# A selective scan and a routed expert block on one core: dt's softplus moved out of PSUM, convolution taps on VectorE in three chunks, and a new interleaving of the steps

## What is computed

```python
xz = x @ W_in.T;  xc, z = split(xz)
xconv = xp[:, :-2]*conv_w[:,0] + xp[:, 1:-1]*conv_w[:,1] + xp[:, 2:]*conv_w[:,2]
xs = silu(xconv);  x_dbl = xs @ W_x.T            # dt_param 64, Bp 16, Cp 16
dt = softplus(dt_param @ W_dt.T + b_dt) + 1e-5
s_t = exp(-exp(A_log) * dt) * s_{t-1} + Bp * dt * xs     # 256 channels x 16 states
out = ((Cp @ W_C.T) * s_t.sum(-1) + D_param * xs) @ W_out.T * silu(z)
```

## Time and profile before

| what | value |
|---|---|
| median of 3 runs | 1205.05 us |
| the profiled execution, its own time | 1197.84 us |
| its span, first to last instruction | 1196.0 us |
| mean granted TensorE clock | 0.907 |
| scans of chunk 0 begin, scans of chunk 7 end | 36.1 us, 658.0 us |
| busy: PE, DVE, ACT, POOL | 85%, 56%, 54%, 57% |

### The profile page before, as it was taken

One profiled execution on the slowest core, in us unless ns is written; L12 is line 12 of the kernel. 1 busy time (PEld: TensorE's weight loads), 2 busy tenths in 40 slices (PEclk: granted clock), 3 DMA queues, 4 the chain that ended last, 5 costly groups with the idle time before them and its releaser, 6 DMA issues.

```text
span 1196.0 us, 15402 instructions
## 1 busy us (share of the span) xinstructions
PE 1013.7 (85%) x4654; PEld 821.6 (69%) x4654; DVE 670.1 (56%) x1152; ACT 643.6 (54%) x1238; POOL 685.4 (57%) x666
## 2 busy tenths in 40 slices
PE   5437497878876878977988899999999999999996
PEld 3204265656655656765776678889999999998885
DVE  6999997998998989955995332100110000110332
ACT  4776769777486695667754443233333333333342
POOL 0696958777489897598696447453243333322221
PEclk9667588898787988898998999999999999999998
DMA  9110100202002016121464659598999988863511
GB/s 293 57 36 1 61 11 18 71 12 77 1 18 71 1 45 221 45 75 62 112 195 110 181 139 237 103 295 247 358 358 332 291 278 264 271 181 62 176 62 53
DMA packets 141636, 163.91 MB, mean 137 GB/s; under 512 B 26345, under 2 KB 126977, under 8 KB 141537
## 3 DMA queue, kind: packets, MB, share of 16 engines
q1 hardware_dynamic: 125872, 144.20, 37.2%
q0 software_dynamic: 15680, 18.72, 8.2%
HBM read 136.57 MB, written 26.74 MB: 137 GB/s over the span
## 4 chain that ended last, share of the span: by engine, by line
PE 49%; POOL 13%; DVE 13%; issue 12%; ACT 7%; SPq 2%; DMA 2%; DVEq 0%; POOLq 0%; ACTq 0%
PE psum L1107 21%; PE psum L1074 9%; PE psum L1063 6%; PE psum L1086 6%; POOL Ssum L1700 6%; DVE S L1292 6%; POOL list_d L1719 2%; DVE psum L1267 2%; ACT A L1570 2%; PE psum L948 1%; PE psum L1050 1%; PE psum L1009 1%; DMA bb<-b 1%; PE psum L1029 1%; POOL xs L1675 1%
## 5 line engine op out<-in xcount | busy, mean ns | idle before, releaser
L1700 POOL TENSOR_TENSOR Ssum<-Ssum,S 128x512 f32<-128x512 f32 x240 | 303.6, 1284 | 89.2 <-DVE S L1292 88.3
L1107 PE MATMUL psum<-w,hT 128*128 128x256 f32 x1136 | 257.1, 384 | 11.7 <-issue 9.2
L1107 PEld LDWEIGHTS psum<-w,hT 128*128 128x128 f32 x1136 | 216.5, 193 | 43.0 <-issue 10.6
L1750 POOL DMA_INDIRECT acc_d<-y,ID x71 | 112.5, 1584 | 231.8 <-DMA acc_d<-y,ID 115.1
L1570 ACT ACTIVATE A<-dts,nea 128x512 f32<-128x512 f32 x256 | 175.0, 717 | 73.8 <-DVE S L1292 61.7
L1074 PE MATMUL psum<-XT,w 128*128 128x256 f32 x800 | 186.1, 390 | 12.5 <-issue 6.2
L1267 DVE TENSOR_TENSOR psum<-us,psum 128x512 f32<-128x512 f32 x256 | 163.3, 683 | 52.1 <-PE psum L993 51.6
L1074 PEld LDWEIGHTS psum<-XT,w 128*128 128x128 f32 x800 | 154.9, 195 | 40.7 <-issue 10.7
L1292 DVE TENSOR_TENSOR_SCAN S<-A,carry,psum 128x512 f32<-128x512 f32 x120 | 148.6, 1266 | 0.0
L1063 PE MATMUL psum<-nT,s 128*128 128x256 f32 x512 | 134.7, 421 | 10.8 <-DVE nb L1305 10.3
L1292 DVE TENSOR_TENSOR_SCAN S<-A,psum 128x512 f32<-128x512 f32 x120 | 141.2, 1206 | 2.4 <-POOL Ssum L1700 2.3
(11 more groups left out here) (162 smaller groups left out, 1222.9 us busy)
## 6 DMA issues: line engine op xcount, KB each, us to landing
w<-W SPq DMA_DIRECT2D x92, 1024.0 KB, 7.0
bb<-b SPq DMA_DIRECT2D x46, 128.0 KB, 8.0
xnb<-x SPq DMA_DIRECT2D x16, 256.0 KB, 3.0
Xr<-x SPq DMA_DIRECT2D x16, 256.0 KB, 4.6
x_d<-gb SPq DMA_DIRECT2D x8, 512.0 KB, 2.9
xn_d<-nb SPq DMA_DIRECT2D x8, 512.0 KB, 3.3
X<-x_d SPq DMA_DIRECT2D x16, 256.0 KB, 7.8
ACC<-acc_d SPq DMA_DIRECT2D x16, 256.0 KB, 5.0
```

Source lines behind the costliest of these rows:

```text
L1107: t = eng.matmul(bank(g)[:, 256 * k:256 * k + 256], hT[n % 2][:, f, 128 * k:128 * k + 128], w[:, f, :], start=f == 0, stop=f == 7)
L1700: eng.tensor_tensor(to, to, of, ALU.add).then_inc(nsum, 1)
L1750: eng.indirect_dma_start(acc_d, bass.IndirectOffsetOnAxis(ap=ID[:, col, 1:2].bitcast(u32), axis=0), y[n % NY][:, k, :], None, compute_op=A ...
```

## The change

Seven edits, made together:

1. `prep` begins 3 slots before the end of the chunk before (FIRST_PREP = -3) and has one yield more between `silu` and `dbc`. In chunk 2's list, silu goes from slot 11 to 9 and dbc from 15 to 14; the beside gelu goes from slot 8 to 4.
2. Softplus works in SBUF (tile `us`), so `dt_out` gives the two banks back at slots 19 and 20. ScalarE adds 1e-5 there in an extra Identity per half.
3. `dt_sum` of chunks 1 to 7 goes from VectorE to GpSimd.
4. The taps of chunks 5, 6 and 7 are added by VectorE out of PSUM; ScalarE's two extra copies and GpSimd's two additions per half fall away there.
5. `low_out` and the steps by it are moved: softplus directly behind `low`, `low_out` three slots later, behind `nT_out`.
6. The scratch of `top2`, `weigh` and `place` lies in the PSUM bank that `count` uses, taken from `top2` on; weigh and place have one instruction more each.
7. `room()` lets an `up` through with 3 of 5 banks open; `table` steps take 1.5 slots instead of 2 while the scans run; "beside" gets 58 calls instead of 54.

Where the steps stand then: before, 18 groups have their gelu ahead of `direct()` and the tiles t8 to t12 run in it; now 19, and t9 to t12. Of the `up` and `down` steps, 14 more stand ahead of the last scan, all of them in chunks 5 to 7.

The 24 table steps have two pairs of scatters among them, where they had one pair of gathers and one of scatters. The diff, cut to its core:

```diff
-FIRST_POST, LAST_POST, FIRST_PREP, LAST_PREP = 0, 27, 0, 27
+FIRST_POST, LAST_POST, FIRST_PREP, LAST_PREP = 0, 27, -3, 27
...
     def room():
 
-        while len(open_uses) > room_for[0] - (2 if past[0] else 3):
+        while len(open_uses) > room_for[0] - 2:
             yield
...
             say("xc_out", i, 0, x0)
             yield
             say("z", i, 0, z0)
-            say("conv", i, 0, x0)
+            if not conv_by_dve(i):
+                say("conv", i, 0, x0)
             say("xc_out", i, 1, x1)
             yield
             say("z", i, 1, z1)
-            say("conv", i, 1, x1)
+            say("conv", i, 0 if conv_by_dve(i) else 1, x0 if conv_by_dve(i) else x1)
             say("z_out", i, 0, z0)
             yield
+            if conv_by_dve(i):
+                say("conv", i, 1, x1)
             say("z_out", i, 1, z1)
             yield
             say("silu", i)
+            yield
             yield
             yield
             yield
@@ -185,28 +189,27 @@
         say("dt", i, 1, t1)
         if i:
             say("dt_out", i, 0, t0)
+            yield
+            say("dt_out", i, 1, t1)
             say("mid_out", i)
-            yield
-            say("low", i)
-            say("dt_out", i, 1, t1)
         else:
             say("mid_out", i)
             say("dt_out", i, 0, t0)
             say("dt_out", i, 1, t1)
-            say("low", i)
-        yield
-        say("softplus", i, t0, t1)
+        yield
+        say("low", i)
+        say("softplus", i)
+        yield
+        yield
+        yield
         say("low_out", i)
...
             say("load_x", i + 1)
         if not i:
             say("stats_x", 6)
-        for c, t in enumerate((t0, t1)):
-            say("dt_sum", i, c, t)
+        for c in range(2):
+            say("dt_sum", i, c)
             say("u", i, c)
...
-        say("top2", r)
+        g = next(use)
+        say("top2", r, g)
         yield
         if not past[0]:
         say("soft", r)
-        g = next(use)
         say("count", r, g)
         yield
         yield
-        say("weigh", r)
+        say("weigh", r, g)
         say("place", r, g)
         yield
...
         for n in range(2 * len(ROUND[r])):
...
             if not past[0]:
                 yield
-                yield
-            elif n % 2:
+            if n % 2:
                 yield
...
+    ahead, done_prep = prep(1), 0
+
+    def prepare(k):
+
+        nonlocal done_prep
+        want = min(n_prep, -(-n_prep * (k + 1 - FIRST_PREP) // (LAST_PREP + 1 - FIRST_PREP)))
+        part(ahead, want - done_prep)
+        done_prep = max(want, done_prep)
+
     for i in range(NC):
-        ahead = prep(i + 1) if i + 1 < NC else iter(())
         behind = post(i - 1) if i else iter(())
-        done_post = done_prep = 0
+        done_post = 0
         for k, _ in enumerate(main(i)):
             tick()
             if k >= FIRST_POST:
                 want = min(n_post, -(-n_post * (k + 1 - FIRST_POST) // (LAST_POST + 1 - FIRST_POST)))
                 part(behind, want - done_post)
                 done_post = max(want, done_post)
-            if k >= FIRST_PREP:
-                want = min(n_prep, -(-n_prep * (k + 1 - FIRST_PREP) // (LAST_PREP + 1 - FIRST_PREP)))
-                part(ahead, want - done_prep)
-                done_prep = max(want, done_prep)
+            if k == LAST_PREP + 1:
+                part(ahead, 99)
+                ahead, done_prep = prep(i + 2) if i + 2 < NC else iter(()), 0
+            if k <= LAST_PREP or k >= 32 + FIRST_PREP:
+                prepare(k if k <= LAST_PREP else k - 32)
             part(routing, 1)
             if i:
 
-                calls = 54 if listed[0] else 26
+                calls = 58 if listed[0] else 26
                 part(beside, calls * (k + 1) // 32 - calls * k // 32)
         part(behind, 99)
-        part(ahead, 99)
...
-TAKING = {"xT", "nT", "xc", "z", "dbc", "dt", "cmat", "wout", "logit", "count", "turn", "up", "down"}
-GIVING = {"xT_out", "nT_out", "xc_out", "z_out", "dbc_out", "dt_sum", "yadd", "gated", "lg_out",
+TAKING = {"xT", "nT", "xc", "z", "dbc", "dt", "cmat", "wout", "logit", "top2", "count", "turn", "up", "down"}
+GIVING = {"xT_out", "nT_out", "xc_out", "z_out", "dbc_out", "dt_out", "yadd", "gated", "lg_out",
           "place", "turn_out", "up_out", "down_out", "weighed"}
 
-TOP, WEIGH, PLACE = 14, 3, 7
+BY_DVE = {0, 5, 6, 7}
+
+
+def conv_by_dve(i):
+    return i in BY_DVE
+
+
...
     if step == "dt":
-        return "dt_done", 2 * i + n + 1
+        return "dt_out", 4 * i + 2 * n if i else n + 1
...
+        def scratch(r, g):
+
+
+            w, b = len(ROUND[r]), bank(g)
+            ranks, eq, oh1 = (b[:, 8 * w * n:8 * w * (n + 1)].rearrange("p (j e) -> p j e", e=8) for n in range(3))
+            mx, ix = (b[:, (24 + n) * w:(25 + n) * w] for n in range(2))
+            return w, ranks, eq, oh1, ohs[:, 0:w, :], mx, q2[:, 0:w], ix
 
...
-                        p = xs[0][:, c, :]
-                        eng.wait_ge(xc_out, taps(0, c))
+                    if conv_by_dve(i):
+                        p = xs[i % 2][:, c, :]
+                        eng.wait_ge(xc_out, taps(i, c))
                         eng.scalar_tensor_tensor(p[:, 1:512], bank(g)[:, 0:511], cw[:, c, 0:1], p[:, 1:512],
                                                  ALU.mult, ALU.add).then_inc(conv, 1)
-                        eng.wait_ge(conv, 2 * c + 1)
+                        eng.wait_ge(conv, 4 * i + 2 * c + 1)
                         eng.scalar_tensor_tensor(p[:, 0:511], bank(g)[:, 1:512], cw[:, c, 2:3], p[:, 0:511],
                                                  ALU.mult, ALU.add).then_inc(conv, 1)
                 elif step == "dbc_out":
@@ -1250,10 +1267,11 @@
                     if i == 0:
...
                 elif step == "dt_sum":
-                    i, c, g = a
-                    eng.wait_ge(softp, 4 * i + 3 + c)
-                    eng.scalar_tensor_tensor(dts[i % 2][:, c, :], bank(g), 1e-5, dts[i % 2][:, c, :],
-                                             ALU.add, ALU.add).then_inc(dt_done, 1)
+                    i, c = a
+                    if i == 0:
+                        eng.wait_ge(softp, 3 + c)
+                        eng.scalar_tensor_tensor(dts[0][:, c, :], us[0][:, c, :], 1e-5, dts[0][:, c, :],
+                                                 ALU.add, ALU.add).then_inc(dt_done, 1)
...
+                    r, g = a
+                    w, pr, eq, oh1, oh2, mx, m2, ix = scratch(r, g)
+                    logits = lg[:, ROUND[r].start:ROUND[r].stop, :]
                     eng.wait_ge(lg_out, ROUND_END[r])
                     if r:
                         eng.wait_ge(soft, r)
+                    if BEFORE[g] is not None:
+                        name, value = BEFORE[g]
+                        eng.wait_ge(emptying[name], value)
                     one(top, eng.memset(M[:, w, :], 0.0))
-                    best(logits, mx, oh1[:, 0:w, :], w)
-                    one(top, eng.scalar_tensor_tensor(pr[:, 0:w, :], oh1[:, 0:w, :], -3e38, logits, ALU.mult, ALU.add))
-                    best(pr[:, 0:w, :], m2, oh2[:, 0:w, :], w)
-                    one(top, eng.tensor_tensor(M[:, 0:w, :], oh1[:, 0:w, :], oh2[:, 0:w, :], ALU.add))
-                    one(top, eng.tensor_tensor(dd[:, 0:w], m2[:, 0:w], mx[:, 0:w], ALU.subtract))
+                    for score, m, oh in ((logits, mx, oh1), (pr, m2, oh2)):
+                        if oh is oh2:
+                            one(top, eng.scalar_tensor_tensor(pr, oh1, -3e38, logits, ALU.mult, ALU.add))
+                        one(top, eng.reduce_max(m, score, axis=AX.X))
+                        one(top, eng.tensor_tensor(eq, score, over_e(m, w), ALU.is_equal))
+                        one(top, eng.tensor_tensor(eq, eq, over_j(iom8, w), ALU.mult))
+                        one(top, eng.tensor_reduce(ix, eq, axis=AX.X, op=ALU.min))
+                        one(top, eng.tensor_tensor(oh, over_e(ix, w), over_j(iom8, w), ALU.is_equal))
+                    one(top, eng.tensor_tensor(M[:, 0:w, :], oh1, oh2, ALU.add))
+                    one(top, eng.tensor_tensor(dd[:, 0:w], m2, mx, ALU.subtract))
                     assert done[top] == TOP * (r + 1)
                 elif step == "weigh":
...
                         eng.activation(dts[i % 2][:, c, :], ps, ACT.Relu, bias=bdt[:, c:c + 1]).then_inc(dt_out, 1)
-                        eng.wait_ge(dt_out, 4 * i + 2 * c - 1)
                     else:
                         eng.wait_ge(relu, c + 1)
-                    eng.activation(ps, ps, ACT.Abs, bias=bdt[:, c:c + 1]).then_inc(dt_out, 1)
+
+                    eng.activation(us[i % 2][:, c, :], ps, ACT.Abs, bias=bdt[:, c:c + 1]).then_inc(dt_out, 1)
                 elif step == "softplus":
-                    i, *gs = a
-                    for c in range(2):
+                    i, = a
+                    first = 6 * i - 2 if i else 0
```

(19 more changed lines are left out.)

67 lines of the change are left out of this document (29 added, 38 removed).

## The result

The changed kernel takes **1235.59 us** (median of 4 runs, 1235.36 to 1236.01), the kernel before beside it 1205.18 us. The ratio is 1.0231, with a 95% interval of 1.0203 to 1.0259: slower, where 1201.5 us was forecast, and outside the range. The profiled execution of the changed kernel has a span of 1234.0 us, that of before 1196.0 us, so 38.0 us have to be found.

A forecast was written before the change was run, and what follows sets the result against it. VectorE bounds 94 to 392 us, VectorE and TensorE are both dense to 659, TensorE is never long without work from 715. Chunks -20.5 plus after the last scan +17 gives -3.5: 1201.5 us, range 1185 to 1221.

The forecast's parts named there:

- costed at nothing: Chunks: GpSimd's prep additions and slot-26 `dt_sum` cost nothing, some 6 us to spare; uncovered, 10 us over chunks 0 to 3.
- Waits gone in chunks 2 to 4, -16.4: Chunks 2 to 4: TensorE's waits for SiLU and nT, with spreads behind them, go; 16.4 us gained.
- `dt_sum` off VectorE, -5.0: Preps of chunks 1 to 4: VectorE loses two `dt_sum` operations of 0.63 us each; 5.0 us gained.
- VectorE's taps, +5.1: Preps of chunks 5 to 7: four tap additions of 0.74 us replace `dt_sum` on VectorE; 5.1 us lost.
- Scratch in PSUM, -7.3: Small VectorE operations with operands in PSUM are no longer held up by GpSimd's SBUF additions; 7.3 us gained.
- Tile work, +3.1: Chunks 5 to 7: 14 more up and down steps, half added, half the waits gone; 3.1 us lost.
- rival 1: Chunks 5 to 7 become TensorE's: 14 us lost instead of 3.1, 1212.4 us in all; chance 0.30.
- the 2.66 us per switch: ScalarE's table loads: quoted skill figure with drain, against 1.28 us; one more gelu block would hold ScalarE 2.8 us longer.
- After the last scan, +17: After the last scan: more matmuls before `count` start the second half of round 2's first half-tile pair 17 us later.
- -20.5 in the chunks: Sum of all chunk terms: -5.0 + 5.1 - 16.4 - 7.3 + 3.1 us.
- The signs named for "wrong": Last scan later than 645 or before 625 us; border waits on `us` or `dts`; round 2 tiles under 125 us after it.
- Rival 3: Chunks: the new spacing fails, dbc waits again, 12 of the 16.4 us stay, 1213.5 us; chance 0.12.

The follow-up runs named there:

- experiment 1: Changed kernel with FIRST_PREP back at 0, so the next preparation no longer begins three slots early; 1218.66 us, ratio 1.0190.
- experiment 5: The changed kernel measured again without an edit; 1237.26 us, 1.0351 of the kernel before.
- experiment 4: Changed kernel with `dt_sum` of chunks 1 to 7 back on VectorE, softplus still in SBUF; 1226.75 us.
- experiment 12: experiment 1 with three banks left free again while scans run, still 58 steps and the table's 1.5 slots; 1230.34 us, ratio 1.0185.
- experiment 10: experiment 9 with `dt_sum` on VectorE again; 1206.49 us, ratio 1.0072.
- experiment 3: Changed kernel with the taps of chunks 5, 6 and 7 back on GpSimd; 1236.25 us.
- experiment 13: experiment 9 with the taps of chunks 5 to 7 back on GpSimd; 1212.98 us, ratio 1.0040.
- experiment 9: Changed kernel with FIRST_PREP at 0 and the old paces of tiles (54 steps, three banks free) and table (2 slots); 1202.70 us, ratio 1.0053.
- experiment 6: Changed kernel with the paces of tiles (54 steps, three banks free) and table (2 slots a step) as before; 1211.68 us.
- 11: Kernel before, changed only so that preparations begin three slots earlier (FIRST_PREP = -3); 1222.36 us, ratio 1.0219.
- 7: Changed kernel with the last chunk's post put ahead of the tile work after the last scan; 1215.76 us, ratio 1.0179.
- 14: Changed kernel: FIRST_PREP 0, last post ahead of tiles, three post steps at once after the last scan, routed scatters held back; 1195.24 us, ratio 0.9886.
- experiment 2: Changed kernel with only the tile work's rule as before: 54 steps a chunk, three banks left free; 1240.72 us.
- experiment 15: experiment 9 with three last-post steps issued at once after the last scan and routed scatters held back; 1226.07 us, ratio 1.0159.

## Why the prediction was wrong

By its own steps, in microseconds of the profiled executions:

- **The step that failed** is the last of the list on the chunks, "costed at nothing": that GpSimd's `dt_sum` stands at slot 26, decays at 28, norm and first transpose at 31, "so there are some 6 us". The queue was named in the right order, but slots were taken for time on GpSimd. In chunk 4 the sum came 12.1 us behind the scan of its slot, after table steps that the step does not name, and the first decay 9.23 us late; in the other chunks it came 2.5 to 3.0 us behind. The early start itself was costed at nothing as well, and experiment 1 puts its price at 18.6 us of the kernel's time (last scan 19.6 us earlier than in experiment 5), experiment 4 that of the late sum beside it at 10.5. The figure named in case the cover was gone, 10 us over chunks 0 to 3, was too small, because it counted GpSimd's own time and not what queues behind it, and left out chunks 4 to 7.
- The mechanism named in that step is not all of the 19.6 us. Chunks 0 to 5 give 13.4 of them, with the transposes' waits in chunk 0 and at the borders to chunks 1 and 5. Another 7.0 are chunks 6 and 7 together, where the trace shows `down` matmuls waiting for gelu, a wait for which the prediction has no term. (The scans begin 0.8 us later in experiment 1.)
- *Waits gone in chunks 2 to 4, -16.4.* The stall before SiLU is gone from TensorE (22.9 to 0.0). Without the early start chunks 2 and 3 are 67.6 and 73.8 us, where 66 and 73 were forecast; in the changed kernel itself they are 69.5 and 75.3. The cause was half right: of the three that were named (SiLU two slots earlier, dbc one, gelu four) experiment 12 shows that gelu's place does it. Chunk 4 gave only 0.4 us (78.7 against 79.1).
- *`dt_sum` off VectorE, -5.0.* Chunks 0 and 1 of experiment 1, which have it, take 57.5 and 65.5 us against 58.0 and 65.5: 0.5 instead of 2.5. In experiment 10 it is worth 3.7 us of the last scan's time over seven preparations.
- *VectorE's taps, +5.1.* Nothing that shows (experiment 3: 1.0 us; experiment 13: -1.1 us in chunks 5 to 7).
- *Scratch in PSUM, -7.3.* The small operations of rounds 0 and 1 together take 21.4 us instead of 29.1 (sums of their durations): 7.7 us, near the forecast. The operation that took 5.87 us takes 0.23, the cast 0.17 instead of 1.93. Whether the time on VectorE reached the chunk's end no run shows. One operation was still held up, and it is one with both operands in SBUF:

```profile
495.82 0.17 DVE L1406 TENSOR_TENSOR e<-e,C 128x8 f32<-128x8 f32 x1
496.02 2.63 DVE L1407 TENSOR_TENSOR_SCAN e<-C,e 128x8 f32<-128x8 f32 x1
...
496.74 1.87 POOL L1739 TENSOR_TENSOR Ssum<-Ssum,S 128x512 f32<-128x512 f32 x1
```

  It ends at 498.65, GpSimd's addition at 498.61. That agrees with what the Trainium skill says on its page "SBUF — State Buffer", section "Who interferes with whom", of a VectorE instruction with two inputs from SBUF: it is shut out until GpSimd's has finished. In the kernel before the hold was longer than any one instruction of GpSimd: the 5.87 us end at 463.64, 0.09 us behind a run of six GpSimd operations without a pause (456.18 to 463.55), of which none takes longer than 1.3 us.
- *Tile work, +3.1.* Experiments 1 and 9 differ in nothing else but the paces: 12.9 more steps, chunks 5 to 7 274.8 instead of 271.7 us, 3.1 more. With one bank less of room (experiment 12) 11.1 more steps cost 11.1 us, near the 14 of rival 1. The agreement is in part luck: the term was the middle between two far ends, and beside the early start the same steps cost more (286.4 us in experiment 5, 270.7 in experiment 6). A table load took 1283 ns on the mean in both traces, and ScalarE's next operation began some 0.01 us behind nearly every one of them: no further stop at a switch shows, so the 2.66 us per switch that the prediction quotes is not what these traces have.
- *After the last scan, +17.* 18.0 measured. The order decides it, as forecast, with 124 listed matmuls before `count`. But that the size fits is partly luck: `count` ended 23.6 instead of 18.5 us later, and the table began 78.7 instead of 73 us after the last scan. The gather of t13's tokens began 21.4 us later (126.0 against 104.6 us after the last scan), its first up step only 17.0, because before TensorE was busy with other tiles until 776.43, when the tokens had been asked for since 762.62. TensorE stood still for 45 us at t13 (39.26 and 5.75).
- The sum without the early start and with all other terms would have been -20.5 in the chunks; experiment 1 shows 653.8 - 658.0 = -4.2. Of these 16.3 us, some 2.6 are chunks 2 and 3, 2.0 chunks 0 and 1, 2.3 chunk 4, and the rest, some 9.5, chunks 5 to 7, where experiment 9 is 5.7 us longer than before with 0.7 steps more. GpSimd's queue at the start of chunk 7 (5.97 us) is one part of that that can be seen; the rest was not taken apart. From -20.5 to the +20.0 of the profiled changed kernel it is 40.5 us: these 16.3, the 19.6 of the early start, and 4.6 by which two executions of the changed kernel differ there.
- The signs named for "wrong" were the right ones: last scan later than 645 us, and a wait at the borders on `us` or `dts` from GpSimd. Rival 3 names the earlier input norm and GpSimd's longer dt, but has them only keep 12 us of a gain and adds no loss, which is why the range missed.

Shown by an edit are the price of the early start (1, 11), that of the late sum beside it (4), gelu's place in chunks 2 and 3 (12), and the chain after the last scan (6, 7, 14). Only read from traces are GpSimd's backlog with the table steps as the reason of the late sum, the waits for gelu in chunk 6, and the share of chunks 5 to 7. Why experiment 2 is 29 us slower than 6 is shown as to the table's pace, argued as to the choking.

## What to carry to other kernels

Slots of a plan are not time: an engine that does all additions in order runs behind its slots, and a step that is "placed early enough" on it is late by its whole backlog (12.1 us in chunk 4, where small scatters shared the queue, 2.5 to 3.0 in the others); look in the trace at when it runs, and at what stands behind each instruction that will wait for it. Before a stage is begun earlier, ask which in-order queues it now enters ahead of urgent work. And tile work that is pulled into a dense stage pays only when the chain that runs after it is shortened as well: here it cost 3.1 us, and left TensorE idle for over 50 us until the last post was put first.

## What was not expected of the hardware

- The kernel before took 1205.2, 1195.5, 1196.1, 1197.3 and 1207.8 us in the five timings, the changed one 1235.6 and 1237.3 in the first and third. The ratio of the two moved from 1.0231 to 1.0351. The last four timings were on different chips; that the chip is the cause was not tested.
- In experiment 15 TensorE issued matmuls one by one for some 20 us, with pauses up to 2.31 us for which the profile names no releaser, and the granted clock of 740 to 770 us was 0.66. The pauses came first, from 744.7 us on: the clock was 1.00 (2.4 GHz) to 749.2 us and 0.50 (1.2 GHz) from there to 769.7. The ninth kernel, with nearly the same steps there, has 1.00 and no such pause. The five runs agree within 0.3%, so it is no chance event of the time, though only one was profiled. The cause is open.

```profile
747.31 0.46 PE L1136 MATMUL psum<-w,hT 128*128 128x256 f32 x1 [1.05 <-issue]
750.08 1.01 PE L1136 MATMUL psum<-w,hT 128*128 128x256 f32 x2 [2.31 <-issue]
```

```profile
740.00:770.00 30.00, 18.43 (x52) 11.61 (x51) 0.69 (x1) 3.89 (x10) 18.63 (x18) 0.66 0.34 57
```
